# Softmax sums of a causal attention layer taken out of the attention loop, and a longer cadence of score and context matmuls

## What is computed

```python
q, k, v = jnp.split(jnp.einsum('bsd,de->bse', x, Wqkv), 3, axis=-1)
q = _layernorm_scale_only(q, q_ln_scale)
k = _layernorm_scale_only(k, k_ln_scale)
...
scores = jnp.einsum('bshd,bthd->bhst', q / jnp.sqrt(jnp.float32(HEAD_DIM)), k)
scores = jnp.where(causal, NEG_INF, scores)
attn = jax.nn.softmax(scores, axis=-1)
ctx = jnp.einsum('bhst,bthd->bshd', attn, v)
out = jnp.einsum('bsd,de->bse', ctx.reshape(B, S, D_MODEL), out_W)
...
h = jax.nn.silu(g) * u
return jnp.einsum('bsi,hi->bsh', h, Wd)
```

## Time and profile before

| | us |
|---|---|
| median of 3 runs | 2299.28 (2298.51 to 2304.28) |
| profiled execution | 2299.23, span 2297.4 |
| stage before attention | 314 |
| attention | 1159 |
| output projection and FFN | 824 |

### The profile page before, as it was taken

The page is one execution under the profiler, slowest core; times in us unless marked ns, Lnnn a source line. Parts: engine busy times, 40 slices in busy tenths (PEclk is TensorE's granted clock), DMA queues, the critical chain, the costliest instruction groups (busy, mean ns, idle before and its releaser), DMA issues.

```text
span 2297.4 us, 35243 instructions
## 1 busy us (share of the span) xinstructions
PE 2270.1 (99%) x12422; PEld 1423.2 (62%) x12422; DVE 1746.0 (76%) x1796; ACT 1360.0 (59%) x2790; POOL 299.0 (13%) x323
## 2 busy tenths in 40 slices
PE   9999999999999999999999999999999999999997
PEld 7888854444444444444444444488888888888886
DVE  7777769999899998989989899945655556565554
ACT  4444479999999999999999999611111111101111
POOL 2111112211112111221111211000000000000001
PEclk9999989999999999999999999999999999999999
DMA  7768893443914438144391444531102111010100
GB/s 262 260 240 283 275 245 85 123 102 79 183 39 116 104 80 176 43 110 99 82 180 43 108 108 111 193 101 36 56 19 74 38 37 47 29 56 19 37 19 20
DMA packets 133221, 247.89 MB, mean 108 GB/s; under 512 B 15256, under 2 KB 40344, under 8 KB 126880
## 3 DMA queue, kind: packets, MB, share of 16 engines
q1 hardware_dynamic: 125840, 194.72, 30.6%
q0 software_dynamic: 6912, 50.33, 9.5%
q10 hardware_dynamic: 288, 0.52, 0.1%
HBM read 122.83 MB, written 72.37 MB: 85 GB/s over the span
## 4 chain that ended last, share of the span: by engine, by line
PE 83%; DVE 2%; ACT 1%; issue 0%; ACTq 0%; DVEq 0%; POOL 0%; POOLq 0%
PE score L1069 25%; PE ctx_acc L1084 22%; PE slot L1502 20%; PE y L1513 10%; PE slot L1427 3%; PE sums_acc L852 1%; ACT probs L1148 1%; DVE total L1210 1%; PE sums_acc L1092 1%; PE slot L1470 1%; PE y L1427 0%; PE slot L1494 0%; DVE stats L1599 0%; DVE x_late L1744 0%; ACT ctx_out L1133 0%
## 5 line engine op out<-in xcount | busy, mean ns | idle before, releaser
L1148 ACT ACTIVATE probs<-score 128x512 f32<-128x512 f32 (+3 forms) x2304 | 1068.5, 630 | 79.6 <-PE score L1069 69.2
L1210 DVE TENSOR_TENSOR total<-total,probs 128x2048 f32<-128x2048 f32 (+3 forms) x444 | 931.5, 2098 | 84.2 <-ACT probs L1148 35.0
L1069 PEld LDWEIGHTS score<-queries,keys 98*128 98x128 f32 x2300 | 392.7, 189 | 410.3 <-ACT probs L1148 325.9
L1069 PE MATMUL score<-queries,keys 98*128 98x512 f32 (+3 forms) x2300 | 630.6, 404 | 3.3 <-ACTq L1128 3.1
L1578 ACT ACTIVATE hidden<-slot,gate_scale_sb 128x512 f32<-128x512 f32 x128 | 88.2, 689 | 631.9 <-PE slot L1502 628.5
L1084 PE MATMUL ctx_acc<-probs,values 128*32 128x512 f32 (+3 forms) x3584 | 420.9, 561 | 0.0
L1640 DVE SCALAR_TENSOR_TENSOR hidden<-slot,up_scale_sb,hidden 128x512 f32<-128x512 f32 x128 | 96.1, 751 | 252.8 <-ACT hidden L1578 252.8
L1012 POOL TENSOR_SCALAR_AFFINE_SELECT probs<-probs 128x512 f32<-128x512 f32 x128 | 178.9, 1398 | 645.2 <-ACT probs L1148 644.8
L1502 PE MATMUL slot<-xt_hi,w_front 128*128 128x512 f32 x600 | 233.6, 389 | 0.1
L1502 PE MATMUL slot<-xt_lo,w_front 128*128 128x512 f32 x600 | 233.5, 389 | 0.0
L1084 PEld LDWEIGHTS ctx_acc<-probs,values 128*32 128x32 f32 x3584 | 85.4, 108 | 186.5 <-issue 98.3
(11 more groups left out here) (152 smaller groups left out, 2252.3 us busy)
## 6 DMA issues: line engine op xcount, KB each, us to landing
side<-probs POOLq DMA_DIRECT2D x48, 1024.0 KB, 6.9
queries<-q_hi SPq DMA_DIRECT2D x64, 256.0 KB
keys<-k_hi SPq DMA_DIRECT2D x64, 256.0 KB
...
```

The costliest lines, as they stand in the source:

```text
L1069: pe.matmul(bank(v)[:, cut(t):], keys[0:ROWS, kb // ST, h, kb % ST * P:(kb % ST + 1) * P], queries[0:ROWS, q_buffer[ch], h, cut(t):], star ...
L1148: act.activation(probs[:, t % PB, h, cut(t):], bank(v)[:, cut(t):], ACT.Exp).then_inc(exped, 1)
L1210: dve.tensor_tensor(into, into, now, ALU.add).then_inc(added, 1)
```

## The change

1. TensorE makes no sums. `sum_total`, `pe_sums`, `ones`, `take_sums` and `sums_acc` are gone.
2. The chunk's total, 128 keys x 4 heads x 512 queries, goes to DRAM as it is (`store_total`, 1 MB; chunk 0's twice). The aside steps are in chunks 3 to 7, into two alternating buffers, and the fold is an accumulating DMA of `total` into the side buffer, issued by GpSimd at place 4 of the next chunk.
3. The sum over the 128 keys is taken by VectorE from pieces that are read back with query blocks of 64 and heads across the partitions (`piece_load`, runs of 256 bytes): for chunks 0 and 1 in 16 pieces during the last head group, for the other six in four pieces each in the FFN of the chunk before.
4. The bank of `sums_acc` is a seventh score bank, and the middle pattern is four pairs, then two context steps.
5. The order of SP's loads and stores in attention is written out by step.

```diff
-    BANKS = 6
-    PE_SUMS = 5
-    QUEUED = (4, 5, 6)
+    BANKS = 7
+    QUEUED = (3, 4, 5, 6, 7)
     ASIDE_FROM, EVERY, ASIDE_REST = 5, 4, 6
+    FOLD_LAG, SIDE_LAG = 4, 8
+    PIECE_FROM, PIECE_EVERY, PIECE_LAG = 6, 5, 3
...
+    piece_at = [first[QUEUED[1]] + PIECE_FROM + PIECE_EVERY * p for p in range(2 * PIECES)]
...
-        want = 2 * (t + LAG) + 2 if alone else 2 * t + (6, 7, 5)[(place(t) - RUN_FROM) % 3]
+        want = 2 * (t + LAG) + 2 if alone else 2 * t + (8, 6)[(place(t) - RUN_FROM) % 2]
...
+        def wait_total_free(engine, g, ch):
+            if ch >= 2:
+                before, gb = ch - 2, g
+            else:
+                before, gb = NCH + ch - 2, g - 1
...
+            if before in QUEUED:
+                engine.wait_ge(folded, 16 * (NF * gb + folds_before(before) + 1))
+            else:
+                engine.wait_ge(total_stored[ch % 2], total_stores(gb, before))
...
+        def store_total(sp, g, ch):
+            if ch in QUEUED:
+                sp.wait_ge(folded, 16 * (NF * g + folds_before(ch) + 1))
...
+                sp.dma_start(dr["totals"].rearrange("n g k (h q) -> n g k h q", h=HG)[ch, g], sides[ch % 2][:])\
+                  .then_inc(side_stored[ch % 2], 16)
+                return
+            sp.wait_ge(added, NA * g + adds_before(last[ch] + 1) + A_CREDIT)
...
+            for n in (ch,) if ch else (0, NCH):
+                sp.dma_start(dr["totals"].rearrange("n g k (h q) -> n g k h q", h=HG)[n, g], total[:, ch % 2, :, :])\
+                  .then_inc(total_stored[ch % 2], 16)
...
+            def fold(g, ch):
+                pool.wait_ge(added, NA * g + adds_before(last[ch] + 1) + A_CREDIT)
+                pool.wait_ge(side_added, 16 * (NQ * g + queued_before(last[ch])))
...
+                pool.dma_start(sides[ch % 2][:], total[:, ch % 2, :, :], accum_op=ALU.add).then_inc(folded, 16)
...
+                    if ch and place(t) == FOLD_LAG and ch - 1 in QUEUED:
+                        fold(g, ch - 1)
+                    elif g and t == FOLD_LAG:
+                        fold(g - 1, NCH - 1)
...
-                if by_pe(t):
...
-                    for h in range(HG):
-                        ins = pe.matmul(sums[h * HD:(h + 1) * HD, n0:], ones[:], probs[:, t % PB, h, n0:],
-                                        start=opens, stop=False)
...
-                    if t - TOTAL_LAG in last:
-                        sum_total(pe, g, last.index(t - TOTAL_LAG))
...
+            def reduce_piece(p):
...
+                dve.wait_ge(piece_in, 16 * NG * (p + 1))
...
+                dve.tensor_reduce(part[:, k, :], piece[:].rearrange("p k q -> p q k"), AX.X, ALU.add).then_inc(reduced, 1)
...
-                    if t in fold_at:
...
-                        dve.tensor_tensor(total[:, ch % 2, :, :], total[:, ch % 2, :, :], side[:], ALU.add).then_inc(folded, 1)
...
-                    if t - TOTAL_LAG - 1 in last:
-                        take_sums(g, last.index(t - TOTAL_LAG - 1))
+                    if g == NG - 1 and t in piece_at:
+                        reduce_piece(piece_at.index(t))
...
+                        reduce_in = (5, 6, 11, 12) if before else (1, 2, 11, 12)
+                        if after and i in reduce_in:
+                            reduce_piece(n, par, reduce_in.index(i))
+                        if after and i == 13:
+                            invert(n)
```

370 lines of the change are left out of this document (204 added, 166 removed).

## The result

The changed kernel takes 2375.03 us, the median of four runs (2370.89 to 2378.40); the kernel before took 2299.11 beside it. The ratio is 1.032, with a 95% interval of 1.030 to 1.035. The prediction said 2256 us, faster, in a range of 2236 to 2284. The profiled execution lasted 2370.89 us (span 2369.1), 71.7 us more than that of before and 115 us more than the sum of the prediction, which was made against that execution.

What follows compares the result with a forecast made beforehand. The prediction took TensorE, busy 99%, to bound the kernel, with ScalarE 5 to 7% behind in attention. Its terms: 2299.2 - 43.0 - 14.9 + 3 + 8 + 3 + 1 = 2256 us, range 2236 to 2284.

Steps and rivals of the forecast that it cites:

- Sums off TensorE: Attention: dropping 52 blocks of sums from TensorE, 0.86 us each, was to save 43.0 us.
- Runs of four pairs: TensorE in attention: eight scores, then two context steps in 3.91 us, fewer breaks of 0.31 us, saving 14.9 us.
- the runs don't get faster: Rival, attention: ScalarE's pace or bank waits hold two steps at 4.02 us; 2271 us, chance 0.12.
- VectorE, +3: Last head group: 16 reductions of about 1.25 us each make VectorE locally dense; +3 us, bounds 0 and 8.
- The DMA adds: Attention: accumulating adds land in about 7.0 us, some late beside other transfers; 2 us a group, +8, bounds 0 and 33.
- adds become the bound: Rival, attention: chained DMA adds land after 8.9 us or later and become the bound; 2360 us, chance 0.07.
- SP's moved work: SP's queue: new waits stand ahead of weight and context loads with tens of microseconds of lead; no cost.
- The pieces: Piece loads: 4.7 us for 512 KB, hidden by five steps, 9.8 us; no cost.
- late pieces: Rival, last head group: pieces take over 9.8 us and VectorE waits; +43 to 2299 or +75 to 2331, chance 0.07.
- The fold at a group's start: Chunk 1's second VectorE step waits for the previous group's chunk 7 fold; 1 us three times, +3, bounds 0 and 8.
- Tail +1, FFN 0: VectorE's last add delays projection, +1 us; FFN reductions of 2.3 us fit its 3.50 us idle gaps, 0.

Runs made afterwards that it cites:

- the last kernel: The best kernel with TensorE's order of before, one and two score pairs over three steps: 2296.0 us, ratio 0.998.
- the best kernel: Changed kernel with loads spread, four DMA adds in chunk 7, pieces apart in 4 KB runs, later folds, FFN scaling between last adds: 2294.9 us.

## Why the prediction was wrong, by its own steps

Three steps make up some 80 of the 115 us between forecast and result: by the groups 20 for the store behind the loads, 35 for the pieces (3 were reckoned) and 35 for chunk 7 of three groups (6 were reckoned). The rest is the runs' term and small waits in all groups, and is not taken apart.

- **Sums off TensorE, 43.0 us: the size holds where nothing waits, not measured alone.** The rows of the sums are gone. In the last kernel, with the old order on TensorE, chunks 5 to 7 of the second group take 6.6 us less than before; six of the group's 13 blocks of sums stood there, 5.2 us by the term. The whole group takes 282.3 us in place of 289.1, so 6.8 us less where the term said 11, since chunks 1 and 2 are 3.4 us longer.
- **Runs of four pairs, 14.9 us: the cadence right, its worth wrong.** 3.91 us were measured as predicted, but 5.8 us and then 1.2 us of time. The step reckoned TensorE's cadence as the group's although it found ScalarE at 3.8 to 3.9 for the same eight exponentials. The rival *the runs don't get faster* had the worth of the term right, nearly nothing, but not for its reason: two steps at 4.02 were not seen.
- **VectorE, +3: mis-sized.** 1.25 us a reduction came from 512 neighbouring elements; strided it was 1.97. Sixteen times 0.72 is 11.5 us; the runs gave 8.
- **The DMA adds, +8, bounds 0 and 33: with the pieces the step that failed most.** Chunk 7 lost 10 to 12 us over its 62 in each of three groups, 35 in all, before the last group is counted. The step took landings of 7.0 from a trace in which DMA was half idle (0.49) and charged the neighbours at 2 us a group; it knew of the nine stores and the key loads and never added up the engines' work of one chunk against its length, nor asked which adds the key loads would stand beside. That reading, 56 of 62 us and the engines full without a break from 860 to 890 us in the second group, was missing. The rival *adds become the bound* had the mechanism, and its condition (landing over 8.9 us) was met in chunk 7, in the first three groups by two of five adds, and in the last group, not throughout; it got a chance of 0.07.
- **SP's moved work, 0: wrong in kind.** The prediction looked at who stands behind SP's new waits, and only for weight and context loads ("that have tens of microseconds of lead"); SP's order in attention got no term. The 20 us of the first group came from the other side: a new store stands behind old loads, and someone now waits for it.
- **The pieces, 0: wrong.** The 9.8 us allowed were not there: the one buffer is free only behind the reduction before, which leaves 7.8. And the estimate of 4.7 us for a piece of 512 KB is the least that was seen; beside the other transfers pieces took up to 13.6. The rival *late pieces* named the place; 35 us is what the pieces cost there, against 43 in the rival, part of it through VectorE's own time and through the adds.
- **The fold at a group's start, +3: about right.** VectorE waits 7.7 us each time, and chunk 1 took 0.7 to 1.6 us more than before, while chunk 0 took about 1 less.
- **Tail +1, FFN 0: about right for the kernel as changed** (+3 together), for a wrong reason: the reductions took 3.82 us, more than the gap of 3.50, and what hid the rest was not read. With fewer adds by DMA the tail became 8 us.

What stays open: the last group of the best kernel is still 17 to 21 us longer than its neighbours, and I have not taken that apart further than bytes of pieces, reductions and weights together. The edits to the last group were each run once, and their gains (8, 12, 15 and 5 us) overlap. Whether the sums on TensorE, with all mends but theirs, would be faster still was not tried.
